# First two chunks' roots by Newton steps on VectorE, and the last inverse bank moved behind the last transposes back

## The reference, cut to what matters

```python
h = layer_norm(x @ fc0_w + fc0_b, ln0_g, ln0_b)              # (64, 64, 64, 32)
for i in range(4):
    x_ft = rfft2(h)                                          # over rows and columns
    out_ft[:, :, :12, :12]  = einsum('bixy,ioxy->boxy', x_ft[:, :, :12, :12], w1[i])
    out_ft[:, :, -12:, :12] = einsum('bixy,ioxy->boxy', x_ft[:, :, -12:, :12], w2[i])
    h = irfft2(out_ft) + einsum('bchw,oc->bohw', h, conv_w[i]) + conv_b[i]
    h = layer_norm(h over channels, ln_g[i], ln_b[i])        # (h-mu)*rsqrt(var+1e-5)*g+b
    if i < 3: h = gelu(h)
h = gelu(h @ fc1_w + fc1_b); h = gelu(h @ fc2_w + fc2_b); h = h @ fc3_w + fc3_b
```

## Time and profile before

| What | Value |
|---|---|
| Median of 3 timed runs | 4886.96 us (4884.19 to 4889.06) |
| The profiled execution | 4915.42 us, span 4913.6 us |
| PE busy | 4008.5 us (82%) |
| PE weight load busy | 3080.9 us (63%) |
| DVE busy | 2260.9 us (46%) |
| ACT busy | 2096.9 us (43%) |
| POOL busy | 1057.9 us (22%) |
| DMA | 213.28 MB, mean 43 GB/s |

### The profile page before, as it was taken

How to read it: one execution, slowest core, us unless ns; L and a number is a source line. 1 busy time by engine, 2 the same in 40 slices (tenths; PEclk the granted TensorE clock), 3 DMA queues, 4 the chain that set the end, 5 groups by cost and what they waited for, 6 DMA issues and landing times. The chain is left out here.

```text
span 4913.6 us, 101922 instructions
## 1 busy us (share of the span) xinstructions
PE 4008.5 (82%) x39344; PEld 3080.9 (63%) x39344; DVE 2260.9 (46%) x4667; ACT 2096.9 (43%) x3178; POOL 1057.9 (22%) x700
## 2 busy tenths in 40 slices
PE   0189999996899999968999999689999995857268
PEld 0068788842788888427888884278887832853146
DVE  6554443431544345224443442244434422787666
ACT  1254444465544444654443446544444463221113
POOL 0032322321223223212332232223223320000020
PEclk9999999998999999989999999899999997779679
DMA  9501201200022022000210220002102101000000
GB/s 206 159 22 59 79 21 60 79 1 16 21 72 67 21 69 69 1 16 21 79 60 21 75 64 2 15 21 79 60 21 79 59 2 31 1 1 1 0 1 9
DMA packets 168682, 213.28 MB, mean 43 GB/s; under 512 B 156402, under 2 KB 158679, under 8 KB 159874
## 3 DMA queue, kind: packets, MB, share of 16 engines
q1 hardware_dynamic: 166514, 182.84, 12.8%
q10 hardware_dynamic: 1680, 23.60, 1.9%
HBM read 147.28 MB, written 59.12 MB: 42 GB/s over the span
## 5 line engine op out<-in xcount | busy, mean ns | idle before, releaser
L760 POOL TENSOR_TENSOR rstd<-var,mhalf 128x16 f32<-128x16 f32 x320 | 931.2, 2910 | 44.1 <-POOL var L757 4.4
L757 POOL TENSOR_TENSOR var<-ssum,eps 128x16 f32<-128x16 f32 x320 | 69.4, 217 | 2923.9 <-DVE ssum L703 2923.9
L737 ACT ACTIVATE h<-tp,gb 128x512 f32<-128x512 f32 x640 | 553.7, 868 | 297.6 <-PE tp L464 296.1
L703 DVE TENSOR_REDUCE ssum<-sq 128x16 f32<-128x512 f32 x640 | 436.2, 683 | 484.5 <-ACT sq L725 481.0
L508 PE MATMUL main<-fwd_w,pix 128*128 128x96 f32 x4096 | 513.9, 293 | 42.1 <-ACT zq L598 35.1
L508 PEld LDWEIGHTS main<-fwd_w,pix 128*128 128x128 f32 x4096 | 509.6, 209 | 48.8 <-ACT pix L743 40.1
L456 PEld LDWEIGHTS main<-convw,h 128*128 128x128 f32 x3072 | 407.4, 209 | 161.2 <-issue 161.2
L464 PE MATMUL tp<-ident,xn 128*128 128x128 f32 x2560 | 423.6, 292 | 77.5 <-DVE xn L694 71.9
L725 ACT ACTIVATE sq<-main 128x512 f32<-128x512 f32 x480 | 286.5, 599 | 441.2 <-PE main L456 394.3
L456 PE MATMUL main<-convw,h 128*128 (+1 forms) x3072 | 455.7, 300 | 0.0
L423 PE MATMUL aux<-inv_r,yd 96*48 96x64 f32 x8192 | 417.1, 256 | 9.5 <-DVE zq L598 4.5
(11 more groups left out here) (240 smaller groups left out, 5868.6 us busy)
## 6 DMA issues: line engine op xcount, KB each, us to landing
mixw<-mix_scratch SPq DMA_DIRECT2D x16, 4608.0 KB, 17.8
y_scratch<-t_w SPq DMA_DIRECT2D x256, 144.0 KB
yd<-y_scratch SPq DMA_DIRECT2D x32, 1152.0 KB, 7.5
mix_scratch<-mixw SPq DMA_DIRECT2D x64, 288.0 KB, 4.8
mixw<-mix_scratch ACTq DMA_DIRECT2D x1, 4608.0 KB, 13.7
h<-in_L_tok_w1r ACTq DMA_DIRECT2D x6, 576.0 KB, 10.1
h<-in_L_tok_w1i ACTq DMA_DIRECT2D x6, 576.0 KB, 10.4
h<-in_L_tok_w2r ACTq DMA_DIRECT2D x6, 576.0 KB, 18.3
```

The costliest lines, as they stand in the source:

```text
L703: dve.tensor_reduce(ssum[:, c % 4, :], sq[:, c % 2, :].rearrange("p (n c) -> p n c", c=CH), AX.X, ALU.add).then_inc(red_done, 1)
L737: act.activation(out, in_, fn, bias=gb[:, 1, stage:stage + 1] if l is None else gb[:, 1, bass.ds(stage, 1)], scale=gb[:, 0, stage:stage + ...
L760: pool.tensor_tensor(rstd[:, c % 4, :], var[:, c % 4, :], mhalf[:, :], ALU.pow).then_inc(rstd_done, 2)
```

## The change

It has two parts. **(1)** Chunks 0 and 1 of each main stage get their roots by the same nine Newton steps on DVE, right behind reduction 1 (`c == 1`), and POOL leaves them out. `rstd_done` is now raised by 4 at the end of these steps, and a new semaphore `early` orders them. POOL's counts on `var_done` are spread over its other six chunks. **(2)** In layer units bank 7 is issued one step later, behind the last transposes back, and ACT drains it at the end of its main stage. The two waits for the inverse drains leave the start of `pe_forward` and stand in the row transform, ahead of the aux banks (y == 2). The embed stage's row transposes use main 0 and 1 where they used aux 0 and 1.

```diff
+VAR_STEPS = {4: 3, 5: 3, 8: 3, 9: 3, 12: 2, 13: 2}
-        def inv_banks(c):
-            return {..., NCH + 3: (4, 5), NCH + 4: (6, 7)}.get(c, ())
+        def inv_banks(c, turns):
+            return {..., NCH + 3: (4, 5), NCH + 4: (6,) if turns else (6, 7), NCH + 5: (7,)}.get(c, ())
...
         def pe_forward(pe, g, s, u, l, nxt):
             m, n = base_of(g, s, u, l)
-            if nxt is not None:
-                for j in range(2):
-                    pe.wait_ge(inv_free[j], inv_of(g, *nxt) + AX_C)
...
-                        mm = pe.transpose((aux if first else tp)[j][:, 128 * i:128 * i + 128],
+                        mm = pe.transpose((main if first else tp)[j][:, 128 * i:128 * i + 128],
...
+                        if nxt is not None and y == 2 and ap == 0:
+                            pe.wait_ge(inv_free[b], inv_of(g, *nxt) + AX_C)
...
+        def newton_steps(dve, m, c, chain, done, step, last, by):
+            p = slice(c % 4 - 1, c % 4 + 1)
...
         # (the nine instructions that dve_newton had, on slots p, with the semaphore chain)
         def dve_newton(dve, m, c):
+            if c == 1:
+                newton_steps(dve, m, c, early, m, 2, rstd_done, 4)
+            else:
+                newton_steps(dve, m, c, newton, (m - START) * NEWTON_OPS + (START + (c // 4) * 4 * NEWTON_OPS), 4, newton, 4)
...
-                if c % 4 == 3:
+                if c % 4 == 3 or c == 1:
                     dve_newton(dve, m, c)
...
-                                   scale=CH ** -0.5 / (CUBIC if c % 4 >= 2 else 1)).then_inc(sq_full, 1)
+                                   scale=CH ** -0.5 / (CUBIC if c % 4 >= 2 or c < 2 else 1)).then_inc(sq_full, 1)
...
-            if nxt is not None and not turns:
+            if nxt is not None:
                 drain_inverse(act, 1, g, *nxt, 7)
...
-                if c % 4 < 2:
+                if c % 4 < 2 and c >= 4:
                     pool.wait_ge(red_done, m + c + 1)
-                    pool.tensor_tensor(var[:, c % 4, :], ssum[:, c % 4, :], eps[:, :], ALU.add).then_inc(var_done, 2)
+                    pool.tensor_tensor(var[:, c % 4, :], ssum[:, c % 4, :], eps[:, :], ALU.add).then_inc(var_done, VAR_STEPS[c])
```

More of the change, by code:

```diff
@@ L151, in tokenizer @@
         newton_w = sb("newton_w", [128, 4, 16])
-        start = sb("start", [1, 28])
+        start = sb("start", [1, 32])
         fwd_w = sb("fwd_w", [128, 96])
@@ L331, in _ @@
                 mm.then_inc(p_pe, 1)
-        main_full, main_free, sq_full, red_done, var_done, rstd_done, newton, tp_full, tp_free = (
-            sem(n) for n in ("main_full", "main_free", "sq_full", "red_done", "var_done", "rstd_done", "newton",
+        main_full, main_free, sq_full, red_done, var_done, rstd_done, newton, early, tp_full, tp_free = (
+            sem(n) for n in ("main_full", "main_free", "sq_full", "red_done", "var_done", "rstd_done", "newton", "early",
                                   "tp_full", "tp_free"))
@@ L376, in inv_of @@
             return g * (LAYERS * UNITS * AX_C) + stage * (UNITS * AX_C) + (START + u * AX_C)
-        def inv_banks(c):
-            return {NCH - 1: (0,), NCH: (1,), NCH + 1: (2,), NCH + 2: (3,), NCH + 3: (4, 5), NCH + 4: (6, 7)}.get(c, ())
+        def inv_banks(c, turns):
+            return {NCH - 1: (0,), NCH: (1,), NCH + 1: (2,), NCH + 2: (3,), NCH + 3: (4, 5), NCH + 4: (6,) if turns else (6, 7), NCH + 5: (7,)}.get(c, ())
         def turn_of(g, u, l):
@@ L475, in pe_main @@
                 if nxt is not None:
-                    for k in inv_banks(c):
+                    for k in inv_banks(c, turns):
                         pe_inverse(pe, g, *nxt, m, k)
@@ L625, in drain_forward @@
                     copy(eng, j, pv[:, :, :, 4 * k:4 * k + 4].rearrange("p c a r -> p a c r"),
-                         (aux if first else tp)[j][:, :].rearrange("p (r a c) -> p a c r", r=4, a=NA)).then_inc(
+                         (main if first else tp)[j][:, :].rearrange("p (r a c) -> p a c r", r=4, a=NA)).then_inc(
                              aux_free[j] if first else row_free[j], 1)
@@ L652, in drain_forward @@
                 eng.tensor_scalar(yn, ys, -1.0, None, ALU.mult).then_inc(y_ready, 1)
-        def dve_newton(dve, m, c):
[L659 to L679, removed]
@@ new lines, in newton_steps @@
+        def newton_steps(dve, m, c, chain, done, step, last, by):
+            p = slice(c % 4 - 1, c % 4 + 1)
+            v, y, w = (x[:, p, :].rearrange("p k n -> p (k n)") for x in (var, rstd, newton_w))
+            dve.wait_ge(red_done, m + c + 1)
+            dve.tensor_scalar(v, ssum[:, p, :].rearrange("p k n -> p (k n)"), EPS / CUBIC ** 2, None, ALU.add).then_inc(chain, step)
+            dve.wait_ge(main_free, after(m, c, 4))
+            dve.wait_ge(chain, done + step)
+            dve.tensor_scalar(y.bitcast(I32), v.bitcast(I32), -0.5, float(0x5f3759df), ALU.mult, ALU.add).then_inc(chain, step)
+            dve.wait_ge(chain, done + 2 * step)
+            dve.tensor_tensor(w, y, y, ALU.mult).then_inc(chain, step)
+            dve.wait_ge(chain, done + 3 * step)
+            dve.tensor_tensor(w, w, v, ALU.mult).then_inc(chain, step)
+            dve.wait_ge(chain, done + 4 * step)
+            dve.scalar_tensor_tensor(out=w, in0=w, scalar=-10 / 3, in1=w, op0=ALU.add, op1=ALU.mult).then_inc(chain, step)
+            dve.wait_ge(chain, done + 5 * step)
+            dve.scalar_tensor_tensor(out=y, in0=w, scalar=5.0, in1=y, op0=ALU.add, op1=ALU.mult).then_inc(chain, step)
+            dve.wait_ge(chain, done + 6 * step)
+            dve.scalar_tensor_tensor(out=w, in0=y, scalar=-0.5 * CUBIC ** 2, in1=y, op0=ALU.mult, op1=ALU.mult).then_inc(chain, step)
+            dve.wait_ge(chain, done + 7 * step)
+            dve.tensor_tensor(w, w, v, ALU.mult).then_inc(chain, step)
+            dve.wait_ge(chain, done + 8 * step)
+            dve.scalar_tensor_tensor(out=y, in0=w, scalar=1.5, in1=y, op0=ALU.add, op1=ALU.mult).then_inc(last, by)
@@ L745, in act_main @@
                 if nxt is not None:
-                    for k in inv_banks(c - 1):
+                    for k in inv_banks(c - 1, turns):
                         if k % 2:
                             drain_inverse(act, 1, g, *nxt, k)
-            if nxt is not None and not turns:
+            if nxt is not None:
                 drain_inverse(act, 1, g, *nxt, 7)
@@ L754, in pool_main @@
             for c in range(NCH):
-                if c % 4 < 2:
+                if c % 4 < 2 and c >= 4:
                     pool.wait_ge(red_done, m + c + 1)
-                    pool.tensor_tensor(var[:, c % 4, :], ssum[:, c % 4, :], eps[:, :], ALU.add).then_inc(var_done, 2)
-                    pool.wait_ge(var_done, m + 4 * (c // 4) + 2 * (c % 4 + 1))
+                    pool.tensor_tensor(var[:, c % 4, :], ssum[:, c % 4, :], eps[:, :], ALU.add).then_inc(var_done, VAR_STEPS[c])
+                    pool.wait_ge(var_done, m + sum(n for k, n in VAR_STEPS.items() if k <= c))
                     pool.wait_ge(main_free, after(m, c, 4))
@@ L879, in _ @@
                 dve.memset(xs[:, :], 0.0).then_inc(xs_zero, 1)
-                for i, counter in enumerate((*aux_full, *aux_free, *inv_full, *inv_free, *row_full, *row_free, turn_full, turn_free, main_full, main_free, sq_full, red_done, var_done, rstd_done, newton,
+                for i, counter in enumerate((*aux_full, *aux_free, *inv_full, *inv_free, *row_full, *row_free, turn_full, turn_free, main_full, main_free, sq_full, red_done, var_done, rstd_done, newton, early,
                                              tp_full, tp_free, fc1_full, g1_done, fc2_full, g2_done)):
```

## The result

| | median | lowest to highest | runs |
|---|---|---|---|
| before | 4898.9 us | 4884.19 to 4915.61 | 20 |
| after | 4881.65 us | 4875.57 to 4886.13 | 20 |

The account below looks back on a forecast made before the run. TensorE, busy 82% of the span, was taken as the bound, losing time to two repeated waits and the slower clock behind them. Terms -35.1 - 49.9 - 3 + 33 + 26 = -29 us took 4886.96 to 4858; range 4832 to 4893.

Parts of the forecast that it names:

- The moved bank, idle part: Start of the 24 layer-unit forward transforms: PE's 1.45 us wait for ScalarE's drain goes, 35.1 us gained.
- The moved bank, slow stretch: First transform matmuls of the 24 layer units: the slower clock goes with the idling, 49.9 us gained, bounds 0 to 49.9.
- The rival, a stretch drawn by the transposes: At the transforms: transposes and narrow inverse matmuls cause the slow clock, so it stays; +21 us, 4908, chance 0.13.
- The Newton steps, idle part: Main-stage starts: VectorE's added chain delays scale 1 and PE loses that time in full, 33 us lost, bounds 0 to 48.
- the present chain: VectorE's existing second chain at second-unit starts, 0.24 us above 2.51; delay 0.88 if it stays so, 0.75 taken.
- the sum: All terms over the whole kernel: -35.1 - 49.9 - 3 + 33 + 26 = -29 us.
- The slow stretch at the starts: Main-stage starts behind chunk 7's longer wait: 16 further clock steps of 1.63 us, 26 us lost, bounds 0 to 47.
- the last one of the sum: From profile to median: the profile's 28.5 us excess carries over, so 4886.96 - 29 = 4858.

Follow-up runs that it names:

- the two edits apart: Two kernels against before: bank 7 moved with the drain waits kept, 4874.76 us (0.9944); waits moved with bank 7 left in place, 4863.23 us (0.9917).
- the wait moved alone: Before with the two inverse-drain waits moved into the row transform, bank 7 left ahead of the last transposes back: 4863.23 us, 0.9917 of before.
- the bank part alone: Before with bank 7, its waits and the row transposes moved, roots of chunks 0 and 1 left on GpSimd: 4832.28 us, 0.987 of before.
- the late chain: After with the Newton steps of chunks 2 and 3 moved behind the scaling of chunk 1: 4728.93 us, 0.9661 of before.
- the Newton part alone: Before with the Newton steps for chunks 0 and 1 on VectorE, bank 7 and both waits left in place: 4999.68 us, 1.0225 of before.
- the first profile: Profiled execution of the unchanged kernel before that the prediction was made against: 4915.42 us.
- the third: Third profile of the kernel before, no edit: 4888.46 us.
- the first experiments: Early follow-up kernels, each timed beside the kernel before on the same chip; the text does not say which ones are meant.

## Why the prediction was off

- **The moved bank, idle part: right.** 35.1 us forecast, 35.1 gone.
- **The moved bank, slow stretch: right against its own trace.** 49.9 forecast, 397.88 - 348.76 = 49.1 measured. That it goes with the idling is shown by the two edits apart (0.98 us: 22.8 us left; 0.68 us: none). The rival, a stretch drawn by the transposes, is out: with the wait moved alone PE does the same things in the same order as before, the last transposes right ahead of the idling, and only the idling is shorter; all 24 transforms run at 1.00. The Trainium skill (TensorE: Matmul & The Clock Gate, "Part 4: PE-mode transpose") says that transpose mode doesn't count as PE-busy in the same way; nothing of that shows at this place.
- **The Newton steps, idle part: right in kind, too large.** 33 us forecast, 21.8 measured from the bank part alone to after. Second units idle 0.6 us more each (0.75 forecast), last stages 0.8 (0.87), the first layer's first units 0.76 by their windows (0.82). In the second units the present chain did not stay 0.24 longer, which the sum had left half open. The last section says what is known of these longer chains. That the order on VectorE ends the start is shown by the late chain.
- **The slow stretch at the starts: right there, but not all of it.** Over the windows of 24 us the mean clock of the last stages' starts fell from 0.98 to 0.88, which is 20 us of their 8 x 24 (18 forecast), and that of the later layers' first units from 0.79 to 0.765, 5.5 us of as many (8 forecast). But from the bank part alone to after PE's busy time grew by 34.6 us in all, not by 26, so some slower clock fell elsewhere. The two profiles stand 56.4 us apart (4826.6, 4883.0), and the sum had 33 + 26 = 59: that this is so near is luck in part, because the idling was forecast too large and the slower clock too small.
- **The step that failed is the last one of the sum:** the profiled execution "stands 28.5 above the median of the timed runs; the difference carries over". It took -29 from one execution and applied it to a median of three runs. The profiled execution of before (4915.42) lies 16.5 us above the median of 20 (4898.9), that of after (4884.81) 3.2 above its own. These 13.3 us are the difference between 30.6 and 17.3. They are no constant offset that both kernels share. The three profiles of before show what they are likely to be: slow clock, more than half of whose spread (15.9 of 27.1 us) is drawn at a wait that the change removes. The term of 49.9 us should have stood as 34 to 50 by the execution; in the prediction its bounds ran from 0 to 49.9 and the upper end was taken. Against the first profile the bank part alone gains 87.0 us and the Newton part alone costs 80.5; against the third they are 60.1 and 107.4, and the medians gave 62 and 105. No profile was taken of an execution of before near 4898.9, so the 13.3 themselves aren't split up. The baseline was off as well: the median of three timed runs was 4886.96, that of 20 is 4898.9, which makes 12 of the 24 us between 4858 and 4881.65.

What stays open: why more slow clock follows the old wait once the Newton steps are there. That is most of what makes them cost 105 us with the wait and 49 without: 19 to 35 us in the transforms (416.79 against 397.88 and 382.11). Open too is why a start with 2.0 us of idling shows anything from 0.79 to 1.00.

## What to carry to other kernels

Where PE's clock falls behind short waits, a wait can cost itself and as much again, and the second half differs by execution. Size it from several profiles, and hold the profiled execution against a median of many runs before you carry a difference over. Ahead of the transforms here, waits of 0.98 us were followed by slow clock in 12 of 24 units and those of 1.45 in 19 to 24, but those of 0.68 and 0.87 in none; in another kernel this has to be measured again. Work added to an in-order engine at the head of a stage costs what the idling there doesn't hide: 2.5 us of chain made the second scaling 0.6 us later, in each of 12 units. Ask first what order would let the added work pay. Here the same early roots cost 49 us with the next chain between the first two scalings, and earned 66 once that chain stood behind them.

## What the runs showed of the hardware

- Time goes with the granted clock in executions of one kernel: 4883.69 us at 0.913 and 4907.52 at 0.909, in the nine runs of before beside the first experiments. It does so only roughly: the profiled execution of before took 4915.42 us at 0.909, and its second profile 4915.56 at 0.907.
- The same 1.45 us of idling was followed by 0, 1.6 or 3.2 us of loss at the transforms of one kernel (14.50, 16.13, 17.7 us), 0.98 us by a loss in 12 of the 24 units (22.8 us in all), and 0.68 us by none in 24.
- A GpSimd power of 2.91 us and VectorE's chain of small two-input instructions ran side by side. In the trace of before the median from the chain's first step to its last is 2.34 us both for the 137 chains that overlap a power at some point and for the 23 that don't, and the power takes 2.91 to 2.92 us in all 320. 32 chains are longer by 0.23 to 0.38, because one step starts late; all of them overlap a power. But a power isn't needed for it: in after 24 chains are longer, and 20 of them overlap none. They stand at the same places of the stages each time, for instance before in the first chain of all 12 second units, in after in the third of all 12. Their cause isn't known.
